# An LSTM pair with attention and feed-forward: recurrent weights as two float16 parts, one scaled gate product on VectorE, and no passes of zeros

## What is computed

```python
def lstm(x, h0, Wx, Wh, b):                 # h0: 16 x 128, c starts at 0
    xp = x @ Wx + b                         # Wx, Wh: 128 x 512
    for t in range(128):
        a = xp[:, t] + h @ Wh
        i, f, o = sigmoid(a[:, 0:128]), sigmoid(a[:, 128:256]), sigmoid(a[:, 256:384])
        g = tanh(a[:, 384:512])
        c = f * c + i * g
        h = o * tanh(c)
    return all h
x = x + linear_attention(lstm(x, cond, L0_cond_W...))   # scores without softmax, scale 1/sqrt(128)
x = x + relu(lstm(x, cond, L0_cond2_W...) @ W1 + b1) @ W2 + b2
```

## Time and profile before

| what | value |
|---|---|
| median of 3 runs | 467.18 us (462.63 to 467.57) |
| the profiled execution | 466.24 us, of which 464.2 us are its span (first to last instruction) |
| busy, share of the span | PE 441.4 us (95%), PEld 351.3 (76%), DVE 261.0 (56%), ACT 212.0 (46%), POOL 17.1 (4%) |
| F matmul L389 | x510, 99.8 us |
| waits for it | ACT sigmoid of F on PE L389: 162.7 us in 250 waits |
| other waits | DVE ring L755 on ACT tanh of c: 59.9 us in 256 waits |

### The profile page before, as it was taken

The page is one execution under the profiler, slowest core; times in us unless marked ns, Lnnn a source line. Parts: engine busy times, 40 slices in busy tenths (PEclk is TensorE's granted clock), DMA queues, the critical chain, the costliest instruction groups (busy, mean ns, idle before and its releaser), DMA issues.

```text
span 464.2 us, 17097 instructions
## 1 busy us (share of the span) xinstructions
PE 441.4 (95%) x6350; PEld 351.3 (76%) x6440; DVE 261.0 (56%) x1422; ACT 212.0 (46%) x1092; POOL 17.1 (4%) x29
## 2 busy tenths in 40 slices
PE   7999999999999999999999999999999999999997
PEld 5877777777777777777789977777777777777775
DVE  4455555555555555555545656556656656665664
ACT  1444455554455555445535344444444444444443
POOL 6800000000000000000000000000000000000000
PEclk9999999999999999999999999999999999999999
DMA  5001111100111110010000000000000000000000
GB/s 168 7 3 18 17 17 17 17 12 5 17 17 17 17 17 9 8 17 11 11 13 3 7 20 20 17 17 14 3 17 17 17 17 17 11 6 17 17 17 11
DMA packets 11689, 8.12 MB, mean 17 GB/s; under 512 B 1097, under 2 KB 11129, under 8 KB 11674
## 3 DMA queue, kind: packets, MB, share of 16 engines
q1 hardware_dynamic: 10874, 6.17, 6.7%
q0 software_dynamic: 512, 1.22, 0.8%
q10 hardware_dynamic: 288, 0.52, 0.3%
HBM read 2.87 MB, written 1.05 MB: 8 GB/s over the span
## 4 chain that ended last, share of the span: by engine, by line
PE 75%; DVE 11%; ACT 9%; issue 3%; DMA 1%; ACTq 0%; DVEq 0%
PE fobank L389 19%; PE gibank L379 16%; PE fobank L379 9%; DVE cell L752 6%; ACT scan L667 5%; DVE ring L755 4%; ACT cell L674 4%; PE gibank L354 3%; PE gibank L359 3%; PE fobank L354 3%; PE fobank L359 3%; PE bankV L365 2%; PE bankY L533 2%; PE bankV L443 2%; PE bankU L526 2%
## 5 line engine op out<-in xcount | busy, mean ns | idle before, releaser
L389 PEld LDWEIGHTS fobank<-ring,whf 128*128 128x128 f32 x510 | 76.6, 189 | 77.8 <-DVE ring L755 70.3
L664 ACT ACTIVATE fgate<-fobank 128x16 f32<-128x16 f32 x256 | 46.9, 183 | 165.0 <-PE fobank L389 162.7
L389 PE MATMUL fobank<-ring,whf 128*128 128x16 f32 x510 | 99.8, 271 | 15.1 <-DVE ring L755 13.1
L748 DVE TENSOR_TENSOR scan<-fgate,cell 128x16 f32<-128x16 f32 x256 | 45.3, 177 | 86.8 <-ACT fgate L664 84.7
L752 DVE TENSOR_TENSOR_SCAN cell<-scan 128x48 f32<-128x48 f32 x256 | 68.4, 267 | 36.8 <-ACT scan L667 1.3
L379 PEld LDWEIGHTS gibank<-h_hi,wh_parts 128*128 128x128 bf16 x1536 | 78.9, 110 | 0.0
L755 DVE SCALAR_TENSOR_TENSOR ring<-cell,ogate 128x16 f32<-128x16 f32 x256 | 44.6, 174 | 59.9 <-ACT cell L674 59.9
L379 PE MATMUL gibank<-h_lo,wh_parts 128*128 128x16 f16 x1536 | 75.3, 169 | 0.3 <-DVE h_lo L760 0.2
L379 PE MATMUL gibank<-h_hi,wh_parts 128*128 128x16 f16 x1536 | 75.4, 169 | 0.0
L667 ACT ACTIVATE scan<-gibank 128x32 f32<-128x32 f32 x256 | 54.8, 214 | 28.7 <-PE gibank L379 0.8
L379 PE MATMUL fobank<-h_hi,wh_parts 128*128 128x16 f16 x771 | 60.0, 174 | 0.4 <-ACT fgate L664 0.2
(11 more groups left out here) (150 smaller groups left out, 463.2 us busy)
## 6 DMA issues: line engine op xcount, KB each, us to landing
rows_t<-rows SPq DMA_DIRECT2D x16, 128.0 KB
x_rows<-in_x_dram SPq DMA_DIRECT2D x17, 64.0 KB
out_dram<-y_sb SPq DMA_DIRECT2D x16, 64.0 KB
xres<-x2T SPq DMA_DIRECT2D x15, 64.0 KB, 1.9
xin<-x2T SPq DMA_DIRECT2D x14, 64.0 KB, 1.8
w<-in_L_ffn_W_dram POOLq DMA_DIRECT2D x2, 256.0 KB, 3.9
wh<-in_L_cond_Wh_dram ACTq DMA_DIRECT2D x1, 256.0 KB, 2.8
wx<-in_L_cond_Wx_dram ACTq DMA_DIRECT2D x1, 256.0 KB, 3.8
```

The costliest lines, as they stand in the source:

```text
L389: nc.tensor.matmul(step_out(p, t, GF), whf[layer][:], ring[:, (s - 1) % STEPS, :], start=False, stop=True, skip_group_check=True).then_inc ...
L664: nc.scalar.activation(fgate[:], fobank[p][:, NB * t:NB * t + NB], ACT.Sigmoid).then_inc(f_done[layer], 1)
L748: nc.vector.tensor_tensor(out=fc_slots, in0=fgate[:], in1=c_psum, op=ALU.mult).then_inc(fc_done[layer], 1)
```

## The change

- `wh_parts` holds two float16 parts instead of three bfloat16 ones, so a step has 4 + 4 passes for G and I and 2 + 2 for O. `split_wh` has two instructions less (layer 0) and writes the second part straight.
- The scale of h is no longer the constant 2 to the power 15. A power of two is found from the largest absolute weight (`most_of`, `spread_most`, a product on PE `top_product`, `scale_from` with ten small DVE instructions), and weights and h get scales whose product is the constant `Z_UNIT` = 1024. Bias (through `ones` = 1024), x (`xT` times 1024) and h0 carry it too; the sigmoids and tanhs take it back with their `scale`. For layer 1 of the text this is done in the start, for layer 2 behind steps 8, 9 and 12 of layer 1.
- A DVE instruction comes into every step: `ogate_h` = ogate x `unit_fill`, between the scan and `ring`. `ring` and `h_hi` become plain products tanh(c) x ogate_h.
- fc and the tanh of G and I share one semaphore, `scan_inputs`; the tanh of c and ogate_h share `h_inputs`.
- Step 0 of each layer has no passes: F, G, I, O are complete after `initial` or the projection, in the order F, then G and I, then O behind the F sigmoid. Iteration 0 of layer 1 is written out instead of being in the loop.
- In the start, two more `keep_warm` matmuls and a product of zeros over 512 columns instead of 256; the copies of the projections (`keep_proj`) come after ACT's step 0.

```diff
-        wh_parts = [sb(f"wh_parts{n}", [P, 3, 4 * H], bf16) for n in (1, 2)]
+        wh_parts = [sb(f"wh_parts{n}", [P, 2, 4 * H], f16) for n in (1, 2)]
...
         def split_wh(eng, e, layer):
-            e.tensor_scalar(whf[layer][:], w[:, gate_cols(GF)], 1.0 / H_UNIT, None, ALU.mult).then_inc(done, 1)
-            e.tensor_scalar(parts[:, 0, :], w[:], 1.0 / H_UNIT, None, ALU.mult).then_inc(done, 1)
+            e.tensor_scalar(whf[layer][:], w[:, gate_cols(GF)], w_unit(layer), None, ALU.mult).then_inc(done, 1)
+            e.tensor_scalar(parts[:, 0, :], w[:], w_unit(layer), None, ALU.mult).then_inc(done, 1)
             if layer == 0:
+                eng.wait_ge(done, 2)
+                e.scalar_tensor_tensor(out=parts[:, 1, :], in0=w[:], scalar=w_unit(layer), in1=parts[:, 0, :],
                                        op0=ALU.mult, op1=ALU.subtract).then_inc(done, 1)
             else:
+                e.tensor_scalar(wh_rest[:], w[:], w_unit(layer), None, ALU.mult).then_inc(done, 1)
                 eng.wait_ge(done, 3)
+                e.tensor_tensor(out=parts[:, 1, :], in0=wh_rest[:], in1=parts[:, 0, :],
+                                op=ALU.subtract).then_inc(done, 1)
-            eng.wait_ge(done, 3 + layer)
-            e.tensor_copy(parts[:, 1, :], rest[:]).then_inc(done, 1)
-            eng.wait_ge(done, 4 + layer)
-            e.tensor_tensor(out=parts[:, 2, :], in0=rest[:], in1=parts[:, 1, :], op=ALU.subtract).then_inc(done, 1)
...
+            pool.wait_ge(scale_made[1], 1)
+            nc.gpsimd.tensor_scalar(wh[1][:, gate_cols(GG)], wh[1][:, gate_cols(GG)], 2.0, None,
+                                    ALU.mult).then_inc(set2_ready, 1)
+            pool.wait_ge(scale_made[1], SCALED)
+            nc.gpsimd.tensor_scalar(w1[:], w1[:], h_back(1), None, ALU.mult).then_inc(set2_ready, 1)
...
-                        for part in range(3):
+                        for part in range(2):
...
-            nc.tensor.matmul(bankV[:, 0:2 * P], warm_w[:], zeros[:], start=True, stop=True, skip_group_check=True)
+            keep_warm(bankV, 2)
+            nc.tensor.matmul(bankV[:, :], zeros[:, 0:P], warm_x[:], start=True, stop=True, skip_group_check=True)
...
+            for g in GATES[0:3]:
+                bias_gate(0, 0, g)
...
                 project_gate(0, 0, g, xT[:, 0, :])
...
+                last = initial(0, g)
+                if g == GF:
+                    last.then_inc(f_ready[0], 1)
+                    top_product(0, gibank[1][:, 0:P])
+            last.then_inc(gi_ready[0], 1)
+            pe.wait_ge(f_done[0], 1)
+            bias_gate(0, 0, GO)
+            project_gate(0, 0, GO, xT[:, 0, :])
+            initial(0, GO).then_inc(o_ready[0], 1)
...
+            project_gate(1, 0, GF, x2T[:, 0, :]).then_inc(f_ready[1], 1)
+            project_gate(1, 0, GG, x2T[:, 0, :])
+            project_gate(1, 0, GI, x2T[:, 0, :]).then_inc(gi_ready[1], 1)
+            pe.wait_ge(f_done[1], 1)
+            project_gate(1, 0, GO, x2T[:, 0, :]).then_inc(o_ready[1], 1)
...
                                      gibank[p][:, 2 * NB * t:2 * NB * (t + 1)].rearrange("p (g b) -> p g b", g=2),
-                                     ACT.Tanh, scale=0.5).then_inc(gi_done[layer], 1)
+                                     ACT.Tanh, scale=0.5 / Z_UNIT).then_inc(scan_inputs[layer], 1)
...
+            def most_of(layer, loaded):
+                dve.wait_ge(loaded, 16)
+                nc.vector.tensor_reduce(w_most[layer][:], wh[layer][:], axis=mybir.AxisListType.X, op=ALU.max,
+                                        apply_absolute_value=True).then_inc(scale_made[layer], 1)
...
+            def scale_from(layer, top):
+                dve.wait_ge(top_ready[layer], 1)
+                nc.vector.tensor_reduce(w_top[:], top, axis=mybir.AxisListType.X, op=ALU.max
+                                        ).then_inc(scale_made[layer], 1)
...
-                dve.wait_ge(tanh_done[layer], n * 2 + 2)
-                nc.vector.scalar_tensor_tensor(out=ring[:, s, :], in0=tanhc, scalar=H_UNIT, in1=ogate[:],
-                                               op0=ALU.mult, op1=ALU.mult).then_inc(h_ready[layer], 1)
-                nc.vector.scalar_tensor_tensor(out=h_hi[:, s, :], in0=tanhc, scalar=H_UNIT, in1=ogate[:],
-                                               op0=ALU.mult, op1=ALU.mult).then_inc(hi_ready[layer], 1)
+                dve.wait_ge(o_done[layer], n1)
+                nc.vector.tensor_tensor(out=ogate_h[:], in0=ogate[:], in1=unit_fill[layer][:],
+                                        op=ALU.mult).then_inc(h_inputs[layer], 1)
+                dve.wait_ge(h_inputs[layer], n * 2 + 2)
+                nc.vector.tensor_tensor(out=ring[:, s, :], in0=tanhc, in1=ogate_h[:],
+                                        op=ALU.mult).then_inc(h_ready[layer], 1)
+                nc.vector.tensor_tensor(out=h_hi[:, s, :], in0=tanhc, in1=ogate_h[:],
+                                        op=ALU.mult).then_inc(hi_ready[layer], 1)
...
+                if s == 8:
+                    most_of(1, wh2_loaded)
+                if s == 9:
+                    spread_most(1)
+                if s == 12:
+                    scale_from(1, bankU[:, 2 * P:3 * P])
```

More of the change, by code:

```diff
@@ L201, in build, with h_unit, w_unit, h_back @@
         out_tb = out.rearrange("b (c t) d -> c t b d", t=CH)
+        def h_unit(layer):
+            return scale[layer][:, 0:1]
+        def w_unit(layer):
+            return scale[layer][:, 1:2]
+        def h_back(layer):
+            return scale[layer][:, 2:3]
+        def pair_back(layer):
+            return scale[layer][:, 3:4]
         def split_wh(eng, e, layer):
[L205 to L206 removed]
@@ L352, in bias_gate @@
             def bias_gate(layer, p, g):
-                return nc.tensor.matmul(gate_out(p, g), bias[layer][:, gate_cols(g)], moving(ones[:, :], g),
+                return nc.tensor.matmul(gate_out(p, g), bias[layer][:, gate_cols(g)],
+                                        moving(ones[:, :], g),
                                         start=g in (GF, GG), stop=False, skip_group_check=True)
@@ L365, in keep_warm, with initial, top_product, step @@
                     nc.tensor.matmul(bank[:, :], warm_w[:], warm_x[:], start=True, stop=True)
-            def initial(layer):
-                for g in GATES:
-                    nc.tensor.matmul(step_out(0, 0, g), wh[layer][:, gate_cols(g)], h0[:], start=False, stop=True,
+            def initial(layer, g):
+                return nc.tensor.matmul(step_out(0, 0, g), wh[layer][:, gate_cols(g)], h0[:], start=False,
+                                        stop=True, skip_group_check=True)
+                for _ in range(n):
+                    nc.tensor.matmul(bankV[:, :], zeros[:, 0:P], warm_x[:], start=False, stop=True,
                                      skip_group_check=True)
-            def step(layer, s, count, fresh=False):
+            def top_product(layer, out):
+                pe.wait_ge(scale_made[layer], 2)
+                nc.tensor.matmul(out, ones[:], w_diag[:], start=True, stop=True).then_inc(top_ready[layer], 1)
+            def step(layer, s, count):
                 p, t = s // CH, s % CH
@@ L382, in passes @@
                     return last
-                if fresh:
-                    pe.wait_ge(hi_ready[layer], count)
-                    passes(h_hi, [GF]).then_inc(f_ready[layer], 1)
-                else:
-                    pe.wait_ge(h_ready[layer], count)
-                    nc.tensor.matmul(step_out(p, t, GF), whf[layer][:], ring[:, (s - 1) % STEPS, :],
-                                     start=False, stop=True, skip_group_check=True).then_inc(f_ready[layer], 1)
+                pe.wait_ge(h_ready[layer], count)
+                nc.tensor.matmul(step_out(p, t, GF), whf[layer][:], ring[:, (s - 1) % STEPS, :],
+                                 start=False, stop=True, skip_group_check=True).then_inc(f_ready[layer], 1)
                 pe.wait_ge(hi_ready[layer], count)
@@ new lines, in _ @@
+            for s in range(STEPS):
+                if s > 0:
+                    if s == 1:
+                        pe.wait_ge(parts_ready[0], PARTS[0])
+                    step(0, s, s)
+                if s == 13:
+                    pe.wait_ge(scale_made[1], 3)
+                beside1(0, s)
+                if s == 12:
+                    top_product(1, bankU[:, 2 * P:3 * P])
+            with pe.Fori(1, ITER) as i:
+                for s in range(STEPS):
+                    step(0, s, i * STEPS + s)
+                    beside1(i, s)
```

292 lines of the change are left out of this document (176 added, 116 removed).

## The result

| | before | after |
|---|---|---|
| median | 465.58 us (462.63 to 467.57, 4 runs) | 449.93 us (446.56 to 458.48, 4 runs) |
| ratio | | 0.965 (0.957 to 0.973) |
| profiled execution, span | 466.24, 464.2 us | 458.48, 456.4 us |

The forecast was 449.0. The execution that was profiled is the slowest of the four, because the chip ran TensorE at its lower clock for some 50 us of it; the steps outside that stretch are those of the other runs.

A forecast was written before the change was run, and what follows sets the result against it. The G and I passes on PE were taken to bound the step, by only 0.10 us. Terms -18.2 - 0.7 - 0.6 + 0.9 + 1.4 - 0.2 = -17.4 took 466.24 to 448.8, forecast as 449 us, range 441 to 458.

The forecast's parts named there:

- The step: Steady steps of both layers: 0.077 us less each, spacing 1.62 instead of 1.70; 236 steps give 18.2 us less.
- The rival of the hidden instruction: Added VectorE instruction ends under the tanh of c: step 1.60, 23.6 us less, 443.4 us; chance 0.17.
- The 0.10: Passes of G and I in a step: twelve become eight at 25 ns each, at most 0.10 us less.
- float16 weights: Passes on PE: a float16 weight load was taken to cost what a bfloat16 one costs, 25 ns a pass.
- The slower rival that rested on them: Float16 weights load slower: all gain lost from 37 ns a pass, 490 us at 50 ns; chance 0.04.
- Boundary and heavy steps: Layer boundary 0.6 us less without the step of zeros; 13 PE-bound steps 0.7 less through fewer O passes.
- The scales of layer 2: On DVE inside layer 1: reduction behind step 8 costs 0.2, chain behind step 12 costs 1.2; 1.4 us more.
- GpSimd's split: Layer 2's weight split on GpSimd: one tensor_tensor holding up h_lo instead of two, 0.2 us less.
- The start: Before the second step: 2.1 us of work added, 1.2 removed, all at half pace; 0.9 us more, bounds 0 to 2.5.
- The rival's mechanism: GpSimd's tensor_scalar instructions also block two-input DVE ones, in four steps by up to 1 us each: 453 us; chance 0.05.
- The clock: PE's lower clock was not expected: side work and warm matmuls unchanged, step shorter, so PE not idler.
- The slower rival, which I gave 0.03: PE falls to its lower clock, 0.53 us more a step; the gain is gone from 33 such steps; chance 0.03.

The follow-up runs named there:

- e8: After with eight more matmuls of ones in the start and six behind step 13 of layer 1, where PE stood idle; 446.63 us, ratio 0.958.
- e5: After without the added VectorE instruction, its scale put into ring and h_hi as the constant 32.0; 448.17 us, ratio 0.955.
- e7: After with the one semaphore of fc and the tanh of G and I split into two again; 462.16 us, one run.
- e9: After with all scales as constants, so neither the chain of scales nor the added VectorE instruction; 441.06 us, ratio 0.943.
- e2: Before with two of its three bfloat16 parts, the third left out; 458.22 us, ratio 0.982.
- e6: Before with two of its three bfloat16 parts and one semaphore for fc and the tanh of G and I; 439.86 us, ratio 0.944.
- e10: Before with only the semaphores of fc and the tanh of G and I merged into one; 464.10 us, ratio 0.996.
- e11: Before with four idle DVE writes behind step 14 of layer 2, stalling PE; 471.66 us, ratio 1.003.
- e12: Before with four idle DVE writes behind step 14 of layer 2 and six more matmuls of ones beside them; 469.65 us, ratio 1.002.
- e1: After without the added VectorE instruction, its factor read by ring and h_hi as a scalar from a tile; 468.17 us, ratio 1.001.
- e3: After with eight more matmuls of ones in the start, where PE stood idle; 449.96 us, ratio 0.968.
- e4: After without the two added warm matmuls in the start; 451.47 us, no ratio on record.

## Why the prediction was right, and where its steps were not

**The step: right.** 1.62 in both layers, ring 0.04 behind the new instruction, which ends 0.01 after the tanh of c. 236 steps were worked out at 18.2; e8 has 9.0 in the 114 steps of layer 2 and 122 x 0.08 = 9.8 in those of layer 1. The rival of the hidden instruction (1.60, 443.4) was 0.02 off, as it said; e5 is that step.

**A term was missing.** The 0.10 was given to the passes alone, and the merged semaphore got no term. Reading the scan's release in the earlier trace rows as input end + 0.04 left out that with two waits it holds only when the second has long been met. By e7, after without the merge would have steps of 1.66, 236 x 0.04 = 9.4 us more. The number was right because an edit that I didn't price paid for it.

**float16 weights: right**, 25 ns a pass as bfloat16. The slower rival that rested on them falls. The Trainium skill, "TensorE: Matmul & The Clock Gate", section on weight-path perf modes, puts fast weight load on for 128 weights of any type but FP32; the 25 ns agree.

**Boundary and heavy steps: right mechanism.** The boundary gave 0.7 where 0.6 was forecast. The heavy steps gave 0.48 instead of 0.7: the four long ones took 2.49 to 2.52 instead of 2.55 to 2.56, but the first after the boundary rose from 1.71 to 1.86. It is 1.85 to 1.92 in every kernel without the passes of zeros (e9 too, which has neither the chain nor the new instruction) and 1.60 to 1.71 in every kernel with them (e2, e6, e10, e11, e12), so it goes with that edit; by what wait isn't shown.

**The scales of layer 2: right size, +1.4 forecast, 1.33 measured.** Timeline of e8_fill_both behind step 12:

```profile
34.98 0.29 DVE L841 TENSOR_REDUCE w_top<-bankU 128x1 f32<-128x128 f32 x1
35.11 0.18 ACT L744 ACTIVATE fgate<-fobank 128x16 f32<-128x16 f32 x1 [0.72 <-PE fobank L436]
...
36.35 0.21 DVE L860 TENSOR_SCALAR scale<-scale 128x1 f32<-128x1 f32 x1
36.48 0.17 DVE L882 TENSOR_TENSOR scan<-fgate,cell 128x16 f32<-128x16 f32 x1
36.66 1.58 POOL L365 TENSOR_SCALAR w<-w,scale 128x512 f32<-128x512 f32 x1 [7.20 <-DVE scale L860]
36.87 0.53 DVE L888 TENSOR_TENSOR ogate_h<-ogate,unit_fill 128x16 f32<-128x16 f32 x1
...
38.92 1.56 POOL L241 TENSOR_SCALAR wh_parts<-wh,scale 128x512 f16<-128x512 f32 x1
39.35 0.29 DVE L896 TENSOR_TENSOR h_lo<-ring,h_hi 128x16 f16<-128x16 f32 x1
...
42.11 1.15 POOL L249 TENSOR_TENSOR wh_parts<-wh_rest,wh_parts 128x512 f16<-128x512 f32 x1
42.15 1.14 DVE L888 TENSOR_TENSOR ogate_h<-ogate,unit_fill 128x16 f32<-128x16 f32 x1
```

fc comes 1.37 behind the F sigmoid instead of 0.21, so the chain costs 1.16; the reduction of step 8 costs 0.17 (1.79 instead of 1.62).

**GpSimd's split: wrong sign**, -0.2 forecast, +0.6 measured. The same rows: the new instruction takes 0.53 beside a tensor_scalar of GpSimd and 1.14 beside its tensor_tensor. That gives 0.20 + 0.05 + 0.97 in three steps, less the 0.58 that before lost in its two (2.07 and 1.91 us instead of 1.70). The failed step: I took h_lo's 0.17 beside a tensor_scalar for a rule on such pairs, and I counted the tensor_tensor instructions but not how long the new instruction is exposed. What decides is when the DVE instruction begins. In the profiles of after, e1, e3, e4, e5, e7 and e8, 11 instructions of the kinds h_lo and ogate_h began 0.13 to 0.43 us into a tensor_scalar of 1.56 to 1.59 us, and every one of them ended 0.71 to 0.74 into it, whether it took 0.58 or 0.28. Those that began 0.56 us or more into one took 0.15 to 0.18, and those that began within 0.01 of it 0.20. The h_lo of the earlier trace rows began 1.25 us in. Beside a tensor_tensor, the hold lasted to its end (19.43 + 0.62 and 18.87 + 1.16 in the earlier trace rows, 42.15 + 1.14 and 42.11 + 1.15 here). The Trainium skill, "SBUF — State Buffer", "Who interferes with whom", has it that a DVE instruction with two SBUF inputs contends with a GpSimd instruction that reads SBUF. The 0.53 agrees, the 0.15 to 0.18 in the later part of a tensor_scalar don't. The rival's mechanism was there; its price of 4 was not.

**The start: wrong sign, and a term that one profile can't give.** +0.9 forecast, -1.2 in the profile. The work was counted at half pace, but the pace turned to full at 8.7 us there, and in the earlier trace rows only at about 17.7. This isn't the change's doing: e6, with the start of before, turned at 8.7 us too. Kernels with the start of before (e2 and e6 with fewer passes) have their second F sigmoid at 13.33 (e6), 13.52 (e10), 14.70 (e11), 15.87, 15.90 (e2) and 16.66 (e12); those with the start of after at 14.90 (e5), 14.96 (e1), 14.70 and 15.36 (e7), and at 14.08 (e4), 14.97 (e3), 15.48 (e8) and 16.53 (e9) with their edits in it. The first group scatters over 3 us with nearly the same instructions, and its mean is 15.0, as is that of the four with after's own start, so the term can't be told from nothing. Also before, the step at half pace cost 0.53, which the sum left in.

**The clock: the step that failed.** "Side work and warm matmuls per step are unchanged and the step is shorter, so PE is not idler" looked at the steady steps only. The change brings two places where PE has nothing to do, the start (2.0 us) and the chain's step. Behind them came the lower clock, with most steps at 2.27 instead of 1.62, 0.65 us each (e11 and e12 show that such a stall can do it). In the profiled execution that was 219.36 - 206.96 = 12.4 us. In the median it is about 3.5: 449.93 against e8's 446.4 (median of the three at a clock of 1.000), and after's own run with the least of it (mean clock 0.996) took 446.56. The slower rival, which I gave 0.03, is thus real and smaller than its break-even.

**How the sum held.** Without the clock the profile says -19.3, 1.9 better than the sum: start 1.3 better, layer 1 0.4 better, heavy steps and boundary 0.1 worse, layer 2 0.2 and the end 0.1 better. That would be 446.9. The clock took some 3.5 back. 449 was a good number for a sum with one term missing, two of wrong sign, and one cost left out.

**Open.** Why the clock fell in e8's run of 456.94 and in e1's at 266.8 us isn't known. In several profiles of before's form (e6, e10, e11, e12) it dips in the start without any of the stalls above. Runs of the kernel before up to 482 us are not explained; the clock on record for that one is 0.999, but e2's profile has 1.00 where its steps took 2.28, so that figure doesn't clear the clock. Windows of e2_two_bf16_parts:

```profile
24.00:28.00 4.00, 3.85 (x35) 2.52 (x34) 1.84 (x10) 1.32 (x7) 0.00 (x0) 1.00 0.00 2
```

## What to carry to other kernels

When an edit shortens one of two inputs until they tie, look at how the consumer waits: two semaphores that cost nothing while one was early cost 0.06 a step here once both came together, and one counting semaphore took that away. A rare, long piece of work on the chain (a scale worked out once) costs its own time and then, often, the clock of TensorE, which it leaves idle. Give TensorE something to run beside it, which helped in most executions here, or do without it: constants saved 9 us of 450 (ratio 0.943 instead of 0.965), though they suit only weights of the range that is built in. An instruction with a scalar from a tile isn't the instruction with a constant; read each form's own row.

## What was new of the hardware

- A scalar_tensor_tensor of 128x16 with its scalar in a tile takes 0.23 us, and the next follows after 0.15; with a constant 0.17 and 0.09 (e1, e5).
- A DVE instruction behind two waits started 0.09 to 0.10 after both inputs ended together, behind one wait 0.04 (e2, e7; e6, after).
- Behind 1.1 to 2.3 us of idle PE (e5, e1, e4, e3, e11, e7, after) the granted clock fell, in e3 for 3 us, in e11 for 14, in after for 51 and in e1 for 58 of nearly unbroken PE work. With 1.24 to 1.62 us of it in the starts of e1, e5 and e4 it did not, and in e1 it also fell with no idle time over 0.17 us.
- Two-input DVE instructions of 128x16 that began 0.13 to 0.43 us into a GpSimd tensor_scalar of 1.56 to 1.59 us were held until 0.71 to 0.74 us of it had passed, those that began 0.56 us or more into one not at all; beside a GpSimd tensor_tensor they were held to its end.
- The clock column shows 1.00 from the first instruction on, while PE's pace is half until 8.7 us (after), 17.7 (before) or about 31 (e2). In a start, only the spacing of the matmuls tells the pace.
